# Rows scaled on VectorE, their high part made straight from the unscaled rows, and two small steps moved to other heads

## The reference, cut to what matters

```
# layer 1: adapter, weights generated for each batch
Wd_b = Wd + dWd ; Wu_b = Wu + dWu
x = x + relu(x @ Wd_b.T + bd) @ Wu_b.T + bu
# layer 2: attention, 16 heads of 16, then a gated feed-forward
rms(x)  = x * rsqrt(mean(x * x) + 1e-6)
h       = gamma * rms(x) + beta          # gamma, beta: one number a column and batch
x = x + alpha * (softmax(q k.T / 4) v) Wo.T     with q, k, v = h Wq.T, h Wk.T, h Wv.T
x = x + f_alpha * swiglu(gamma_f * rms(x) + beta_f)
```

## Time and profile before

| | |
|---|---|
| median of 3 runs | 1081.57 us (1075.45 to 1085.4) |
| profiled execution, its own time | 1075.05 us |
| its span | 1073.2 us |
| granted TensorE clock, mean | 0.992 |
| TensorE busy | 1024.5 us, 95% of the span |
| VectorE busy | 748.3 us, 70% |
| ScalarE busy | 643.2 us, 60% |
| GpSimd busy | 174.9 us, 16% |
| chain that ended last | TensorE 65%, VectorE 13%, issue 7%, ScalarE 4%, GpSimd 2% |

### The profile page before, as it was taken

How to read it: one execution, slowest core, us unless ns; L and a number is a source line. 1 busy time by engine, 2 the same in 40 slices (tenths; PEclk the granted TensorE clock), 3 DMA queues, 4 the chain that set the end, 5 groups by cost and what they waited for, 6 DMA issues and landing times.

```text
span 1073.2 us, 15997 instructions
## 1 busy us (share of the span) xinstructions
PE 1024.5 (95%) x5149; PEld 629.7 (59%) x5149; DVE 748.3 (70%) x1199; ACT 643.2 (60%) x879; POOL 174.9 (16%) x203
## 2 busy tenths in 40 slices
PE   7999999999999999999999999998999999999996
PEld 5776767777543343434344343432477777887784
DVE  5867668887867777776877777777855466556654
ACT  5456323343367777787787877676753555555545
POOL 0000001221131333232332333020311000000000
PEclk9999999999999999999999999999999999999998
DMA  9968633225443453635345363533210000000001
GB/s 275 384 185 239 184 80 106 40 63 168 79 150 75 128 139 79 185 77 168 82 139 137 81 171 77 190 70 103 86 33 1 20 1 20 20 20 13 8 20 39
DMA packets 92041, 110.92 MB, mean 103 GB/s; under 512 B 47185, under 2 KB 57425, under 8 KB 90961
## 3 DMA queue, kind: packets, MB, share of 16 engines
q1 hardware_dynamic: 60736, 100.56, 32.2%
q10 hardware_dynamic: 31248, 9.65, 5.0%
HBM read 65.81 MB, written 33.03 MB: 92 GB/s over the span
## 4 chain that ended last, share of the span: by engine, by line
PE 65%; DVE 13%; issue 7%; ACT 4%; POOL 2%; DVEq 0%; DMA 0%; ACTq 0%; POOLq 0%; SPq 0%
PE st_ps L1737 13%; PE mx_ps L1737 7%; PE st_ps L1593 7%; DVE mx L1178 6%; PE gate_ps L1455 6%; PE av_ps L1577 6%; PE val_ps L1455 6%; PE misc_ps L1511 4%; PE misc_ps L1613 3%; PE misc_ps L1626 3%; PE mx_ps L1535 2%; PE y_ps L1465 2%; DVE stage L1187 2%; PE misc_ps L1617 2%; POOL m_lo L652 1%
## 5 line engine op out<-in xcount | busy, mean ns | idle before, releaser
L1178 DVE TENSOR_REDUCE mx<-mx_ps 128x1 f32<-128x512 f32 x488 | 314.8, 685 | 116.6 <-PE mx_ps L1535 116.4
L1535 PE MATMUL mx_ps<-kring,qring 48*128 48x512 f32 x500 | 196.8, 457 | 9.8 <-DVE mx L1178 6.1
L1593 PE MATMUL st_ps<-qring,kring 50*128 50x512 f32 x512 | 187.8, 445 | 6.8 <-ACT shared L901 3.6
L1593 PEld LDWEIGHTS st_ps<-qring,kring 50*128 50x128 f32 x512 | 77.7, 184 | 156.0 <-issue 114.1
L901 ACT ACTIVATE pbuf<-st_ps 128x1024 f32<-128x1024 f32 x128 | 129.5, 1022 | 46.8 <-PE st_ps L1593 44.4
L901 ACT ACTIVATE shared<-st_ps 128x1024 f32<-128x1024 f32 x128 | 129.1, 1024 | 41.1 <-PE st_ps L1593 39.5
L1535 PEld LDWEIGHTS mx_ps<-kring,qring 48*128 48x128 f32 x500 | 83.4, 184 | 42.0 <-DVE mx L1178 38.1
L1349 DVE TENSOR_TENSOR shared<-st_ps,shared 128x512 f32<-128x512 f32 x64 | 44.2, 690 | 81.6 <-PE st_ps L1737 63.0
L1025 ACT ACTIVATE p_hi<-shared 128x512 fp32r<-128x512 f32 x64 | 40.4, 632 | 71.9 <-DVE shared L1349 71.3
L1235 DVE SCALAR_TENSOR_TENSOR h<-val_ps,r,gelu 128x1024 f32<-128x1024 f32 x32 | 41.1, 1283 | 47.4 <-PE val_ps L1455 47.4
L1358 DVE TENSOR_TENSOR p_lo<-shared,p_hi 128x512 fp32r<-128x512 f32 x64 | 47.0, 734 | 37.7 <-ACT p_hi L1025 37.0
(11 more groups left out here) (237 smaller groups left out, 2058.0 us busy)
## 6 DMA issues: line engine op xcount, KB each, us to landing
chunk<-in_gen_w SPq DMA_DIRECT2D x8, 2048.0 KB, 8.7
qring<-q_parts SPq DMA_DIRECT2D x64, 192.0 KB, 3.6
kring<-k_parts SPq DMA_DIRECT2D x64, 192.0 KB, 4.6
q_parts<-stage SPq DMA_DIRECT2D x16, 512.0 KB, 2.8
k_parts<-stage SPq DMA_DIRECT2D x16, 512.0 KB, 2.8
xres<-in_xT SPq DMA_DIRECT2D x8, 512.0 KB, 11.5
shared<-in_x SPq DMA_DIRECT2D x8, 512.0 KB, 12.5
q_parts<-stage SPq DMA_DIRECT2D x16, 256.0 KB, 3.0
```

The lines of the kernel that those rows point to most:

```text
L1178: nc.vector.tensor_reduce(mx[h // GH % 2][:, col:col + 1], mx_ps[:, qt % 2], AX, ALU.max).then_inc(S["mx_free"], 1)
L1535: nc.tensor.matmul(out, qring[h // GH][r:r + QROWS, h % GH // 2, qt * P:(qt + 1) * P], kring[h // GH][r:r + QROWS, h % GH // 2, :], start= ...
L1593: ins = nc.tensor.matmul(st_ps[half][:, kt % 2], kring[g][r:r + SROWS, i % GH // 2, kt * P:(kt + 1) * P], qring[g][r:r + SROWS, i % GH // ...
```

## The change

For turns 2 and later (`rows_by_two`), ScalarE no longer scales `hf` in place. It writes `m_hi` straight from the unscaled rows with gamma and beta as scale and bias; VectorE then scales and shifts `hf` in place, ahead of its maxima of step 0, each half after ScalarE has read it; and GpSimd waits for VectorE's result before it subtracts. The copy of `hf` to `m_hi` behind head 0's exponentials goes. The root `rn` moves ahead of the exponentials of step 14. The second root moves from step 15 to step 9 of the next turn. `g_hi` and `g_lo` move from step 1 to step 4.

```diff
+        def rows_by_two(j):
+            return not (isinstance(j, int) and j < 2)
...
# GpSimd
                 if i == 0 and has_p:
                     for k in range(KD):
-                        wait(pool, "h_hi", KD * p + k + 1)
+                        wait(pool, "h" if rows_by_two(j) else "h_hi", KD * p + k + 1)
                         sub(m_lo[:, k], hf[:, k], m_hi[:, k].bitcast(F32)).then_inc(S["h_lo"], 1)
...
-                if i == 1 and has_a:
+                if i == 4 and has_a:
                     wait(pool, "g_hi", a + 1)
                     sub(g_lo[:], one(gen, a).rearrange("p a n -> p (a n)"), g_hi[:].bitcast(F32)) \
                         .then_inc(S["g_lo"], 1)
...
# ScalarE
+            def log_rows(f):
+                log_mean(one(gen, f).rearrange("p a n -> p (a n)"), misc[:], "sumf_ps", f + 1, "lnf")
             def inverse_root(f):
-                log_mean(one(gen, f).rearrange("p a n -> p (a n)"), misc[:], "sumf_ps", f + 1, "lnf")
+                log_rows(f)
                 root(one(gen, f).rearrange("p a n -> p (a n)"), f + 1, "lnf", "rf")
...
-                if i == 0 and has_p and not opens:
+                if i == 0 and has_p and rows_by_two(j):
+                    for k in range(KD):
+                        wait(act, "t", KD * p + k + 1)
+                        nc.scalar.activation(m_hi[:, k], hf[:, k], ACT.Identity,
+                                             scale=cv[:, C_GA, k, bass.ds(p, 1)],
+                                             bias=cv[:, C_BA, k, bass.ds(p, 1)]).then_inc(S["h_hi"], 1)
+                elif i == 0 and has_p and not opens:
                     scale_rows()
...
                 if i == 14 and has_a:
                     log_mean(rn[:], misc[:], "suma_ps", a + 1, "lna")
+                    root(rn[:], a + 1, "lna", "rn")
                 if i == 15 and has_f and not behind(j):
-                    inverse_root(f)
+                    if isinstance(j, int) and j > NB:
+                        inverse_root(f)
+                    else:
+                        log_rows(f)
                 if has_b:
                     ...  the step's two exponentials
-                if i == 0 and has_p:
+                if i == 0 and has_p and not rows_by_two(j):
                     for k in range(KD):
                         wait(act, "h", KD * p + k + 1)
                         copy(m_hi[:, k], hf[:, k]).then_inc(S["h_hi"], 1)
-                if i == 1 and has_a:
+                if i == 9 and (not isinstance(j, int) or 3 <= j <= NB):
+                    root(one(gen, f - 1).rearrange("p a n -> p (a n)"), f, "lnf", "rf")
+                if i == 4 and has_a:
                     act.wait_ge(A["gend"], a + 1 if isinstance(a, int) else NB)
                     wait(act, "l1u_ps", 2 * a)
                     copy(g_hi[:], one(gen, a).rearrange("p a n -> p (a n)")).then_inc(S["g_hi"], 1)
-                if i == 14 and has_a:
-                    root(rn[:], a + 1, "lna", "rn")
...
# VectorE
+                if i == 0 and has_p and rows_by_two(j):
+                    for k in range(KD):
+                        wait(dve, "h_hi", KD * p + k + 1)
+                        nc.vector.tensor_scalar(hf[:, k], hf[:, k], cv[:, C_GA, k, bass.ds(p, 1)],
+                                                cv[:, C_BA, k, bass.ds(p, 1)], ALU.mult, ALU.add) \
+                            .then_inc(S["h"], 1)
                 early = 1 if i in (1, 2, 10) else 2
                 take_maxima(maxima[:early])
```

## The result

The changed kernel takes **1106.94 us** (median of 4 runs, 1101.34 to 1109.33) against 1083.49 for the kernel before in the same comparison (1075.45 to 1086.66): ratio **1.0255, interval 1.0211 to 1.03**. (The ratio on record is not the quotient of these two medians, which is 1.022; that of the two profiled executions is 1.0245.) The time lies above the forecast of 1090 and outside its range of 1077 to 1099. The profiled execution took 1101.34 (span 1099.3, mean granted clock 0.972, before 0.992), 26.3 more than the profiled one before.

What follows compares the result with a forecast made beforehand. The prediction took TensorE, busy 95% of the span, as bound, with ScalarE fullest at turn boundaries. Later head 2 starts, 5 x 1.85 plus 2.14, added 11.4 us: 1086.5 by the profile, 1093.0 by the median, so 1090, range 1077 to 1099.

Steps and rivals of the forecast that it cites:

- What bounds the boundary: At the turn boundary ScalarE is fullest; head 0's first pair of maxima, done before 478.03, is what the change touches.
- The timeline from A: Boundary of turns 3 to 4, counted from ScalarE's start on m_hi (A, 477.05): second scaling collides with GpSimd, ends A+3.13.
- R: Start of head 0's first maxima reduction on VectorE, forecast at 480.10; before, it started near 476.7.
- The wait's term: Head 2 starts 1.85 us later at five boundaries and 2.14 later at the first, 11.4 us in all.
- Steps that cost nothing: Moved roots, g_hi and g_lo cost nothing; the maxima's split is late by up to 1.3 us but covered until head 8.
- The first rival: VectorE's second scaling starts before GpSimd's subtraction: 5.5 us less over six boundaries, 1080.5 to 1087.0; chance 0.23.
- The boundary holds 1.00 today: Argument against a clock fall: TensorE's granted clock at the turn boundary was 1.00 in the kernel before.
- the chance of 0.10 for the clock: Rival: TensorE's some 2 us stop drops its clock to 1.2 GHz at each boundary, 1110 to 1116 us; chance 0.10.
- The row that spoke for the forecast: A window elsewhere in which TensorE kept 2.4 GHz (granted 1.00) with 1.28 busy of 3 us.
- the row that spoke against it: A window near the end with a mean granted clock of 0.66 at 1.92 busy of 3 us.
- The clock's price: At 1.2 GHz one projecting head (3.9 us) takes twice as long at each of six boundaries: 23 us more.
- two levels: Starting levels for the forecast: profiled execution, giving 1086.5, and median of the runs, giving 1093.0; 1090 was put between.

Runs made afterwards that it cites:

- late: The changed kernel with VectorE's two scalings behind all four of head 0's maxima instead of ahead of them: 1079.34 us against 1079.16 for the kernel before, ratio 1.0016.
- gap: Kernel before with only roots, g_hi and g_lo moved, plus a bare VectorE wait for head 0's first exponential ahead of its maxima: 1105.23 us, ratio 1.0235.
- busy: The changed kernel with eight spare TensorE products into an unread PSUM bank in head 0's second half: ratio 1.012 to the kernel before.
- moves: The kernel before with only the two roots, g_hi and g_lo moved, rows scaled by ScalarE as before: 1078.99 us, ratio 1.0016.
- both: The changed kernel, but GpSimd waits for both scaled halves, so the second scaling meets no subtraction: ratio 1.0258 to the kernel before.
- first: The changed kernel, but VectorE scales each half once GpSimd's product is there, and ScalarE copies m_hi between head 0's exponentials: 1074.54 us against 1081.15, ratio 0.995.
- both_busy: The changed kernel with GpSimd waiting for both scaled halves and five spare TensorE products in the idle time: 1085.64 us, ratio 1.0044 to the kernel before.
- after: The changed kernel itself, with the whole change against the kernel before: 1106.94 us against 1083.49, ratio 1.0255.

## Why the prediction was wrong, point by point

- **What bounds the boundary: right.** The first pair of head 0's maxima, done before 478.03 in the kernel before, is what the change delayed; late and gap show it from both sides.
- **The timeline from A: right to within 0.1.** A came 0.27 earlier (0.30 predicted; value product to `m_hi` 417.01 to 420.16, before 473.93 to 477.35). A scaling alone took 0.55 (0.48). Second scaling behind GpSimd by 0.07 (0.09), ending 0.28 after it (0.28). R = A+3.11 at this boundary (A+3.05). TensorE's product at R+0.74, as taken. The Trainium skill (SBUF — State Buffer, section "SBUF: two separate sides") lets whichever starts first hold the port pair for its whole instruction: the traces agree on who loses, 1.47 for the scaling that came second; and in late, where VectorE came first (the row at 427.20), GpSimd's two subtractions took 2.74 instead of 2.53. How much the loser loses is less clear: there the second scaling ran for 0.38 more beside the first subtraction, which became 0.23 longer.
- **The wait's term, 1.85 a boundary and 11.4 us in all: nearly right,** as far as it goes. Busy shows it alone: 12.9 at six boundaries, less 1.25 in the rest of the turns, is 11.6 in the trace; the comparison gives 13 (1.2%, interval 0.6 to 1.8%). Its head 2 starts at R+6.27 (421.99 to 428.26), 6.28 predicted.
- **Steps that cost nothing: right.** Moves is level with the kernel before, at the wall and at the boundaries; `m_lo` was no longer waited for; head 8 did not wait for its maxima.
- **The first rival, VectorE wins the second half: wrong.** At all six boundaries GpSimd came first, by 0.06 to 0.07, and the second scaling collided as in the forecast. So narrow a lead, derived from sums of small numbers, came out right partly by luck.
- **The failed step: "The boundary holds 1.00 today", and with it the chance of 0.10 for the clock.** The sum kept TensorE at its full clock through an idle time that it had itself worked out at some 2 us; for the clock it held nothing. That the boundary held 1.00 before, with a stop of 0.60, says nothing of one with a stop of 2. The clock fell to its lower level at six boundaries of six, in both with 1.01 to 1.26 us of idle time and in gap with 1.46 to 1.70 too. A sign that the prediction itself named, a clock under 1.00 between 350 and 720 us, came true. The row that spoke for the forecast, 1.28 busy of 3 us at 1.00, was taken from another place of the kernel, with other work ahead of it; the row that spoke against it, 0.66 near the end, got too little weight. And the trace of the kernel before has a stop of nearly the predicted length that the prediction did not look at, in the feed-forward, in otherwise full work. The stop, and the window behind it:

```profile
840.76 0.47 PE L1793 MATMUL av_ps<-sum_lo,mean_r 128*128 128x512 f32 x1 [1.97 <-DVE sum_lo L1353]
...
840.00:850.00 10.00, 9.24 (x34) 7.45 (x35) 5.09 (x8) 4.83 (x7) 0.00 (x0) 0.83 0.01 2
```

These rows alone spoke for a chance well above 0.10. Why the opening holds its clock over such a window no run here settles.
- **The clock's price, 3.9 a boundary and 23 us: too high.** It measured 2.56 and 16. The two five-microsecond windows of the changed kernel, 421 to 431, show a granted clock of 0.82 and 0.50, so 5 x 0.18 + 5 x 0.50 = 3.4 us of full clock are missing; this boundary lost 2.4 by it (16.83 against 14.42 in busy). The rest presumably fell into time in which TensorE waited for VectorE and lost nothing; no run measures that apart. With it, forecast and clock give 1090 + 16 = 1106, and 1106.94 was measured. That this is so close is luck: 1090 was the middle between two levels that lie 6.5 us apart.

## What to carry to other kernels

A wait that is put ahead of the bounding engine's supplier costs more than its length: find out how long TensorE will stand still, compare that with the stop that it has today, with the clock at 1.00, **at that place** (here 0.60; 1.01 was too much), and do not take a thinly filled stretch elsewhere in the kernel as proof that the clock holds. The same work placed where its operand is ready first (first) instead of behind a third engine (the changed kernel) was the difference between 0.5% faster and 2.5% slower. A few spare products into an unused bank (eight and five here) tell wait and clock apart in one run. When two kernels differ by less than one per cent, compare runs of equal mean clock.

## What the runs showed of the hardware

- The granted clock is kept by work that serves nothing: eight products in 2.11 us (busy) or five in 1.42 us (both_busy) brought it back to 1.00 at every boundary, worth 2.56 and 15.57 - 13.46 = 2.11 us a boundary.
- At the lower level the eight value products took 1.91 us against 1.05, and a product of 512 columns 0.79 against 0.49. The level stayed for some 7 us behind the stop (424.01 to 431, where 0.39 is back), although TensorE had few stops in it. At two of the changed kernel's six boundaries it stayed for some 10 us (the boundaries take 16.26 to 17.63).
- The clock fell at 18 of 18 boundaries with a stop of 1.01 to 2.19 us (after, both, gap). Elsewhere a stop of that length can go either way: the 1.97 us in the feed-forward, there in all ten traces, were followed by a fall in six (0.83 in the kernel before) and by 1.00 in four (after, moves, both, busy), and a stop of 1.30 at 760.33 in the kernel before left it at 1.00. What decides there no run here shows.
- Such spells also come around the start of attention in some executions and not in others: in late's profile 0.50 from 300 to 310 us, in both_busy's 0.73 and 0.75 from 340 to 360, in first's none. The runs of the kernel before follow the mean clock in the same way, 1072.83 us at 0.994 and 1083.98 at 0.981; that spread widens every interval here.
